# Cross-attention kernel, single-head stage: order of weight products, transfers, splits and bias sums

## The reference

```python
q = einsum('blh,oh->blo', h_english, w_q)
k = einsum('bsh,oh->bso', h_lojban, w_k)
v = einsum('bsh,oh->bso', h_lojban, w_v)
probs = softmax(einsum('blh,bsh->bls', q, k) / sqrt(h))
context = einsum('bls,bsh->blh', probs, v)
x = h_english + alpha * einsum('blh,oh->blo', context, w_o)
```

## Time and profile before

| | us |
|---|---|
| median of 3 runs | 1885.19 |
| lowest, highest | 1883.24, 1888.57 |
| profiled execution | 1888.23 |
| its span | 1886.3 |
| TensorE busy in it | 1815.4 |
| start of the first centring in it | 149.58 |

### The profile page before, as it was taken

One profiled execution on the slowest core, in us unless ns is written; L12 is line 12 of the kernel. 1 busy time (PEld: TensorE's weight loads), 2 busy tenths in 40 slices (PEclk: granted clock), 3 DMA queues, 4 the chain that ended last, 5 costly groups with the idle time before them and its releaser, 6 DMA issues.

```text
span 1886.3 us, 30413 instructions
## 1 busy us (share of the span) xinstructions
PE 1815.4 (96%) x11396; PEld 1774.0 (94%) x11396; DVE 1137.8 (60%) x2520; ACT 808.4 (43%) x1868; POOL 771.1 (41%) x634
## 2 busy tenths in 40 slices
PE   8878999999999999999998999999999999999999
PEld 4768999999999999999897999999999999999999
DVE  3566556556666565565669655556556556555565
ACT  3424443434444434444364543444435444434354
POOL 2566135243053342421368424244144243352244
PEclk9988999999999999999999999999999999999999
DMA  8842012121021110110362212112012011110132
GB/s 242 213 157 82 26 41 62 36 61 40 12 63 46 46 57 29 57 40 18 117 204 69 70 29 63 29 46 62 18 57 56 25 57 40 46 57 29 43 99 85
DMA packets 73589, 123.79 MB, mean 66 GB/s; under 512 B 13888, under 2 KB 25536, under 8 KB 73444
## 3 DMA queue, kind: packets, MB, share of 16 engines
q1 hardware_dynamic: 71140, 117.64, 21.1%
q10 hardware_dynamic: 2304, 4.20, 0.7%
...
...
## 4 chain that ended last, share of the span: by engine, by line
PE 89%; DVE 6%; issue 2%; ACT 1%; DMA 1%; POOL 1%; DVEq 0%; ACTq 0%; SPq 0%; POOLq 0%
PE psum L563 27%; PE psum L565 27%; PE psum L564 27%; PE psum L808 4%; PE psum L587 2%; DVE ctxT_lo L1252 1%; DVE xT L1435 1%; DVE g_lo L1252 1%; PE psum L686 1%; POOL kw L482 1%; PE psum L774 1%; DMA ctx_rows_in<-ctx_dram 1%; DVE cen L1411 1%; DVE psum L1405 1%; ACT sq L1038 1%
## 5 line engine op out<-in xcount | busy, mean ns | idle before, releaser
L451 POOL TENSOR_TENSOR wbuf_hi<-stage,zero_col 128x512 fp32r<-128x512 f32 x256 | 267.3, 1044 | 928.3 <-PE psum L774 479.6
L498 POOL TENSOR_TENSOR wbuf_lo<-stage,wbuf_hi 128x512 fp32r<-128x512 f32 x256 | 330.0, 1289 | 20.0
L565 PE MATMUL psum<-pT_hi,ctx_rows_lo 121*128 121x250 f32 (+3 forms) x1152 | 332.2, 288 | 0.0
L563 PE MATMUL psum<-pT_hi,ctx_rows_hi 121*128 121x250 f32 (+3 forms) x1152 | 331.6, 288 | 0.0
L564 PE MATMUL psum<-pT_lo,ctx_rows_hi 121*128 121x250 f32 (+3 forms) x1152 | 330.8, 287 | 0.0
L563 PE MATMUL psum<-ctxT_hi,a_hi 128*125 128x362 f32 (+1 forms) x832 | 280.3, 337 | 3.5 <-DVE a_lo L1261 3.5
L565 PE MATMUL psum<-ctxT_hi,a_lo 128*125 128x362 f32 (+1 forms) x832 | 273.1, 328 | 0.0
L564 PE MATMUL psum<-ctxT_lo,a_hi 128*125 128x362 f32 (+1 forms) x832 | 272.7, 328 | 0.0
L1252 DVE TENSOR_TENSOR a_lo<-psum,a_hi 128x500 fp32r<-128x500 f32 (+2 forms) x288 | 146.2, 526 | 208.3 <-ACT a_hi L927 207.6
L563 PE MATMUL psum<-a_hi,wbuf_hi 128*128 128x400 f32 x720 | 253.8, 353 | 4.5 <-issue 4.5
L564 PE MATMUL psum<-a_lo,wbuf_hi 128*128 128x400 f32 x720 | 247.8, 344 | 0.0
...
## 6 DMA issues: line engine op xcount, KB each, us to landing
stage<-head_w_dram SPq DMA_DIRECT2D x256, 256.0 KB, 2.6
...
key_stage<-head_w_dram SPq DMA_DIRECT2D x32, 256.0 KB, 4.5
l0w<-l_w_dram ACTq DMA_DIRECT2D x16, 256.0 KB, 13.4
...
```

Source lines behind the costliest of these rows:

```text
L451: return nc.gpsimd.tensor_tensor(out, in_, zero_col[0:in_.shape[0], :].broadcast_to(tuple(in_.shape)), ALU.add)
L498: nc.gpsimd.tensor_tensor(lo, held, hi.bitcast(F32), ALU.subtract).then_inc(stage_free, 1)
L563: pe.matmul(out, a_h, x_hi, start=start, stop=False)
L565: return pe.matmul(out, a_l, x_hi, start=False, stop=stop)
```

## The change

TensorE multiplies only the first weight pair at the start; the second is made in four groups (`value_weights(g)`), before and after the queries and behind the first two scores, and its splits are spread over ScalarE's and VectorE's lists. SP waits for the first weight piece before x, and for the first pair before the first context; the differences are stored between contexts, keys 0 to 3 are loaded after the second columns, keys 4 to 7 after the last context of turn 0. Second-turn columns follow `ls_mm` two at a time. Sums of keys 0 to 7 stand ahead of the steps. In the steps there are 2, 3, 3, 4, 3, 3 and 3 sums, and three at the end. GpSimd's order and the second turn's splits move accordingly. `prob0` and `w0` get other addresses, in the room of the weight buffers.

```diff
--- before.py
+++ after.py
@@ -176,8 +176,6 @@
-                prob0 = sb("prob0", [P, 2, T], F32, batches)
-                w0 = sb("w0", [P, DC, LAYERS * H], F32, batches)
@@ -209,6 +207,9 @@
         with ExitStack() as before_layers:
             key_stage = sb("key_stage", [P, KEYS, D], F32, before_layers)
+            prob0 = sb("prob0", [P, 2, T], F32, before_layers)
+            sb("before_w0", [P, 2 * D - 2 * T], F32, before_layers)
+            w0 = sb("w0", [P, DC, LAYERS * H], F32, before_layers)
@@ -342,42 +343,62 @@
+            sp.wait_ge(l0w_ld[0], 32)
             sp.dma_start(xT[:, :, :], xT_d[0]).then_inc(x_ld[0], 16)
-            load_ctx_columns(0, 0)
-            load_ctx_rows(0, 0)
...
-            for b in range(1, NB):
-                load_ctx_columns(0, b)
-                load_ctx_rows(0, b)
+            sp.wait_ge(l0w_ld[DC - 1], 32)
+            load_ctx_columns(0, 0)
             sp.wait_ge(diff_s, 1)
             sp.dma_start(diff_d, diff[:, 0, :]).then_inc(diff_out, 16)
+            load_ctx_rows(0, 0)
+            load_ctx_columns(0, 1)
+            sp.wait_ge(diff_out, 16)
+            for i in range(4):
+                load_key_weights(i)
+            load_ctx_rows(0, 1)
+            load_ctx_columns(0, 2)
+            load_ctx_rows(0, 2)
+            load_ctx_columns(0, 3)
+            load_ctx_rows(0, 3)
             sp.wait_ge(dv_lo_s, 1)
             sp.dma_start(dv_d[0].rearrange("(h k) -> h k", k=P), dv_hi[:, :].bitcast(F32)).then_inc(dv_out, 16)
             sp.dma_start(dv_d[1].rearrange("(h k) -> h k", k=P), dv_lo[:, :].bitcast(F32)).then_inc(dv_out, 16)
-            sp.wait_ge(diff_out, 16)
-            for i in range(4):
+            for i in range(4, 8):
                 load_key_weights(i)
+            for b in range(2):
+                sp.wait_ge(ls_mm, b + 1)
+                load_ctx_columns(1, b)
             sp.wait_ge(lw_mm, 8)
             sp.dma_start(x1[:, :, :], xT_d[1]).then_inc(x_ld[1], 16)
...
-            for i in range(4, 8):
-                load_key_weights(i)
-            for b in range(NB):
-                sp.wait_ge(ls_mm, b + 1)
-                load_ctx_columns(1, b)
-                sp.wait_ge(lu_mm, b + 1)
-                load_ctx_rows(1, b)
-                load_key_weights(8 + 2 * b)
-                load_key_weights(9 + 2 * b)
-            for i in range(16, 25):
-                load_key_weights(i)
+            keys = iter(range(8, LAYERS * H))
...
+            def some_key_weights(count):
+                for _ in range(count):
+                    load_key_weights(next(keys))
...
+            sp.wait_ge(ls_mm, 3)
+            load_ctx_columns(1, 2)
+            sp.wait_ge(lu_mm, 1)
+            load_ctx_rows(1, 0)
+            some_key_weights(2)
+            sp.wait_ge(ls_mm, 4)
+            load_ctx_columns(1, 3)
+            sp.wait_ge(lu_mm, 2)
+            load_ctx_rows(1, 1)
+            some_key_weights(3)
+            sp.wait_ge(lu_mm, 3)
+            load_ctx_rows(1, 2)
+            some_key_weights(3)
+            sp.wait_ge(lu_mm, 4)
+            load_ctx_rows(1, 3)
+            some_key_weights(13)
...
-            for i in range(25, LAYERS * H):
-                load_key_weights(i)
+            some_key_weights(3)
@@ -504,25 +525,29 @@
             key_diff()
+            some_key_weights(2)
             ctx_rows_lo(0, 0)
+            some_key_weights(2)
             ctx_rows_lo(0, 1)
+            some_key_weights(2)
             ctx_rows_lo(0, 2)
...
             ctx_rows_lo(0, 3)
-            some_key_weights(6)
+            some_key_weights(8)
             ctx_rows_lo(1, 0)
...
             ctx_rows_lo(1, 1)
-            some_key_weights(3)
             ctx_rows_lo(1, 2)
...
             ctx_rows_lo(1, 3)
-            some_key_weights(LAYERS * H - 18)
+            some_key_weights(LAYERS * H - 23)
...
+                        if ph == 0 and i == WBUFS - 2:
+                            pool.wait_ge(lp_mm, TURNS * NB)
@@ -580,14 +605,19 @@
             def single_head():
...
-                for j in range(2):
+                for c in range(DC):
+                    pe.wait_ge(l0w_ld[c], 32)
+                    for g in range(DC):
+                        mm = pe.matmul(bank[g], chunk(l0w[0][:, c, :], g), l0w[1][:, c, :], start=(c == 0), stop=(c == DC - 1))
+                        if c == DC - 1:
+                            mm.then_inc(lw_mm, 1)
...
+                def value_weights(g):
...
-                        pe.wait_ge(l0w_ld[j * DC + c], 32)
-                        for g in range(DC):
-                            mm = pe.matmul(bank[j * DC + g], chunk(l0w[2 * j][:, c, :], g), l0w[2 * j + 1][:, c, :],
-                                           start=(c == 0), stop=(c == DC - 1))
-                            if c == DC - 1:
-                                mm.then_inc(lw_mm, 1)
+                        pe.wait_ge(l0w_ld[DC + c], 32)
+                        mm = pe.matmul(bank[DC + g], chunk(l0w[2][:, c, :], g), l0w[3][:, c, :], start=(c == 0),
+                                       stop=(c == DC - 1))
+                    mm.then_inc(lw_mm, 1)
...
                 def queries0():
@@ -618,12 +648,16 @@
+                    if g < 2:
+                        pe.wait_ge(lw_lo, DC + g + 1)
...
                 def turn_probs0(g):
...
+                    if g == 0:
+                        pe.wait_ge(lw_lo, DC + 3)
@@ -633,6 +667,8 @@
+                    if g == 0:
+                        pe.wait_ge(lw_lo, 2 * DC)
@@ -647,12 +683,15 @@
+                value_weights(0)
                 queries0()
-                pe.wait_ge(lw_lo, 8)
+                value_weights(1)
...
                 scores0(0)
                 scores0(1)
+                value_weights(2)
+                value_weights(3)
                 for g in range(TURNS * NB):
@@ -981,27 +1019,28 @@
                 act.wait_ge(x_ld[0], 16)
...
                 ctx_columns_hi(0, 0)
+                for g in range(DC):
+                    weights_hi(0, g)
                 ctx_rows_hi(0, 0)
+                weights_hi(1, 0)
                 ctx_columns_hi(0, 1)
-                weights_hi(0)
+                queries0_hi(0)
+                queries0_hi(1)
                 ctx_rows_hi(0, 1)
+                queries0_hi(2)
                 ctx_columns_hi(0, 2)
-                weights_hi(1)
-                queries0_hi(0)
+                queries0_hi(3)
                 ctx_rows_hi(0, 2)
-                queries0_hi(1)
+                weights_hi(1, 1)
                 ctx_columns_hi(0, 3)
-                queries0_hi(2)
-                queries0_hi(3)
-                ctx_rows_hi(0, 3)
                 exp0(0)
...
+                weights_hi(1, 2)
+                ctx_rows_hi(0, 3)
+                weights_hi(1, 3)
                 for g in range(TURNS * NB):
...
-                    if g == 0:
-                        act.wait_ge(x_ld[1], 16)
-                        copy(x1_hi[:, :, :], x1[:, :, :]).then_inc(x_hi_s, 1)
                     if b < 2:
@@ -1009,21 +1048,25 @@
                     rows_of(g)
+                    if g == 1:
+                        act.wait_ge(x_ld[1], 16)
+                        copy(x1_hi[:, :, :], x1[:, :, :]).then_inc(x_hi_s, 1)
+                        ctx_columns_hi(1, 0)
                     if g == 2:
-                        ctx_columns_hi(1, 0)
+                        ctx_columns_hi(1, 1)
                         ctx_rows_hi(1, 0)
                     if g == 3:
+                        ctx_columns_hi(1, 2)
                         queries1_hi(2)
...
-                        ctx_columns_hi(1, 1)
+                        ctx_rows_hi(1, 1)
...
-                        ctx_rows_hi(1, 1)
...
-                        ctx_columns_hi(1, 2)
...
+                    if g == 4:
                         ctx_columns_hi(1, 3)
                         ctx_rows_hi(1, 2)
-                    if g == 4:
+                    if g == 5:
                         ctx_rows_hi(1, 3)
@@ -1333,29 +1375,34 @@
+                nc.vector.memset(prob0[:, :, 0:1], 0.0)
                 ctx_columns_lo(0, 0)
+                for g in range(DC):
+                    weights_lo(0, g)
+                some_key_sums(2)
+                weights_lo(1, 0)
                 ctx_columns_lo(0, 1)
-                weights_lo(0)
+                queries0_lo(0)
+                some_key_sums(1)
+                queries0_lo(1)
+                some_key_sums(2)
+                queries0_lo(2)
                 ctx_columns_lo(0, 2)
-                weights_lo(1)
-                queries0_lo(0)
-                queries0_lo(1)
+                queries0_lo(3)
+                some_key_sums(2)
+                weights_lo(1, 1)
+                maxima0(0)
                 ctx_columns_lo(0, 3)
-                queries0_lo(2)
-                queries0_lo(3)
-                dve.wait_ge(lw_mm, 8)
-                nc.vector.memset(prob0[:, :, 0:1], 0.0)
```

(24 more changed lines are left out.)

14 lines of the change are left out of this document (6 added, 8 removed).

## The result

Before, 1886.88 us (median of 4 runs, 1883.24 to 1888.61); after, 1943.45 us (median of 4, 1939.74 to 1948.00). The ratio is 1.0298, with a 95% interval of 1.0280 to 1.0315: the change makes the kernel 3% slower, by 56.6 us. The prediction of 1938 (1906 to 1953) holds the time, and its case, slower, came.

A forecast was written before the change was run, and what follows sets the result against it. TensorE was busy 96% of the span, but in the single-head stage it waits for low probabilities behind VectorE's and ScalarE's ordered lists. Terms 12.8 + 32.1 - 3.1 + 9.6 + 5.2 - 3.0 = 53.6 us gave 1938 us, range 1906 to 1953.

The forecast's parts named there:

- start: Single-head stage up to the end of step 0's attention: scores wait for key 4's late load and sum; +12.8 us.
- steps 1 to 3: Attention steps of batches 1 to 3: each now contains a whole trip of key loads; 53.6 us against 21.54, +32.1.
- step 4: Fifth attention step: four keys land behind rows, but some second-turn context work is gone elsewhere; 23.9 us against 27.05, -3.1.
- step 5: Sums of keys 20 to 22 precede low probabilities, their products wait behind the third context's rows; 16.5 us, +9.6.
- step 6: As in step 5 with the fourth context, without columns and scaling; 14.3 us against 9.07, +5.2.
- end: Stretch before the first centring: fewer keys and sums remain, so the last residual starts with the last product; -3.0 us.
- to 59.7, which the first scores cover: At the start, the second scores' wait for the second value bank's low part, until 59.7 us, hides behind the first scores.
- trip: Attention ends, SP issues rows and keys, they land, product, sum, low probabilities, attention; loads priced at 6.2 us per MB.
- quick transfers: Rival: same waits, but the queue runs at 318 GB/s; 22 us less, 1916 us; chance 0.15.
- no change: Rival: gains at the start and the end against short trips of about 5 us; 1885 us; chance 0.03.
- the faster case: Rival: keys are ready when VectorE reaches their sums, so the chain of waits is void; 1870 us; chance 0.04.
- Crowding: Rival: every trip takes some 4 us more as second-turn columns, keys and rows meet; 1955 us; chance 0.12.

The follow-up runs named there:

- e10_start: e4_weights_only with splits of the first weights ahead of the first column tile, query parts and second value part ahead of later contexts, on ScalarE and VectorE; 1883.49 us.
- e3_gate: Changed kernel with keys 4 and 5 loaded ahead of the first turn's last rows, columns and rows, and key 6 ahead of the last rows; 1933.40 us.
- e2_keys_first: Changed kernel with SP issuing the keys ahead of the context rows in each of steps 0 to 3, behind the same wait for attention; 1932.15 us.
- e9_split_later: Changed kernel with GpSimd's split of the second turn's first context rows moved behind the products of keys 16 to 19; 1939.48 us.
- e5_rows: Changed kernel with ScalarE making the high parts of the second turn's third and fourth context rows one attention earlier; 1934.24 us.
- e4_weights_only: Changed kernel with most key parts and second-turn contexts ordered as before; first weights alone, four value groups and later x split stay; 1891.33 us.
- e8_groups_first: Changed kernel with all four groups of value weights ahead of the queries, as before the change; 1941.05 us.

## Why the prediction was right

The sum of the prediction was 53.6 us; the trace shows 59.6, and the medians 56.6. By its own terms, forecast and then measured: start +12.8, +17.3; steps 1 to 3 +32.1, +34.5; step 4 -3.1, -4.0; step 5 +9.6, +9.1; step 6 +5.2, +5.4; end -3.0, -2.7.

*The start* had the right mechanism, and its size was off by 4.5 us. The queries began at 28.78 and not at about 25, because the splits of the first weights stood behind the first column tile (with the splits ahead of it, in e10_start, they begin at 23.34); this was not on the path. The scores started at 56.93 (forecast 56.3) and for the reason named; e3_gate shows it. The step that failed is the one behind: "to 59.7, which the first scores cover". The second scores started at 62.40, because GpSimd's split of rows between the products of keys 5 and 6 took 4.91 us where the earlier trace rows has 3.46, and TensorE took 2.8 us for these scores and 7.86 for the two groups where 2.0 and 6.9 were counted, with a granted clock of 0.68 in the first 4 us of it:

```profile
54.80 4.91 POOL L483 TENSOR_TENSOR ctx_rows_lo<-ctx_rows_in,ctx_rows_hi 121x1536 fp32r<-121x1536 f32 x1
```

```profile
62.00:66.00 4.00, 3.60 (x13) 3.08 (x14) 3.43 (x7) 0.65 (x2) 0.16 (x1) 0.68 0.59 183
```

Besides, key 4 lands at another moment in each run: its product began between 51.97 (e2_keys_first) and 57.28 (e9_split_later) with the same instructions ahead of it, and A0 came between 77.8 and 83.3 in the five kernels with this start. So the 17.3 is one draw of a term that varies by 5 us.

*Steps 1 to 3* were forecast at 18.1, 16.9 and 18.6 us and took 16.5, 17.1 and 22.5. The trip itself was right as a sum, from the issue of the rows to the end of the last sum 12.7 us in step 2 (94.61 to 107.34), as forecast, but made up otherwise: the first key's product starts after 8.3 us, and then the three products (3.7), not the transfers, set the pace. That the two agree is partly luck, since the price of 6.2 us per MB was misread. At 64.44 the queue of before had not run empty: keys 6 and 7 had been issued from 62.25 on, more loads followed from 69.89, and between 64.44 and 77.7 not 2.14 but 3.5 MB moved, at 262 GB/s. In the changed kernel the rows and three keys moved between 96 and 104 us at 211 GB/s, which is the 4.7 us per MB of e2_keys_first, so the last of them was there some 9.4 us after the rows were issued and not 10.7, and the pace of the products made up the rest. The column split of step 3, counted at 1.7 from the earlier trace rows, took 4.26 beside GpSimd (e9_split_later), 2.6 of the 3.9 us by which that step was longer than forecast.

*Steps 4, 5, 6 and the end* were each within 1 us. In step 4 the scaling was counted at some 0.6 us where the earlier trace rows shows 2.11; in the changed kernel it took 0.78. At the end the agreement is luck. From A6 to the centring the changed kernel took 21.4 us at a mean granted clock of 0.87 in this trace, while six of the eight other kernels with the same end took 18.9 or 19.0 us at 1.00. Before had 24.2 at 0.91. Against 18.9 the term is -5.3, not -3.0. e5_rows shows the mechanism of steps 5 and 6, the rows behind the copy of an attention. What the prediction did not have is how little of the 13 us on TensorE would reach the end even without the keys: in e4_weights_only none does, and e8_groups_first shows that the groups weigh some 2 us on the path, since value parts are late next.

*The rules weighed.* The estimate of 6.0 us for rows and three keys from the Trainium skill (DMA: Bandwidth & Descriptors, Anatomy of one DMA) would have given 1904; the trace has 8.3 us to the first key's product alone, and the time came 39 us above. Its form, a fixed part and a part by the byte, is nevertheless the one that e2_keys_first supports on this queue.

*The rivals* fall: quick transfers (1916), no change and the faster case (1870) by the 8 to 9 us that each round waits before its first product. (The gain of quick transfers was counted too small: by the prediction's own rates 1.73 MB at 318 GB/s take 5.4 us, 5.3 less than 10.7 and not 3.3, and 2.06 MB 6.3 less than 12.8 and not 4, which gives about 1908.) Crowding (1955) is partly there, in step 3's first key at 9.3 us after the attention against 8.3 in step 2's, but is worth 1 us, not 12.
